# Deferred numerators in a linear-attention phase, and the edges' gathers and scatters regrouped in tiles of 128

## The reference, cut to what matters

```python
# graph attention of layer 0, over 21250 edges (src, dst); 4 heads of 64
xl = (x @ Wl).reshape(n, H, D); xr = (x @ Wr).reshape(n, H, D)
msg = xl[src] + xr[dst]
act = where(msg > 0, msg, 0.2 * msg)
e = einsum('ehd,hd->eh', act, att)          # one score per edge and head
...                                          # softmax over the edges of a node
# mix, 16 heads of 64
q = phi(x @ Wq); k = phi(x @ Wk); v = x @ Wv
kv = einsum('bhtd,bhtm->bhdm', k, v)
num = q @ kv; den = q @ k.sum(t)
out = (num / den) @ Wo
```

## Time and profile before

| | us |
|---|---|
| median of three runs | 3459.63 |
| the profiled execution, its own time | 3469.89 |
| its span in the profile | 3468.2 |
| count, 124 to 402 | 278 |
| mix0, 402 to 938 | 536 |
| out0, 938 to 1172 | 234 |
| mix1, 2221 to 2645 | 424 |
| PE busy over the span | 2749.8 (79%) |
| DVE busy | 1617.4 (47%) |
| POOL busy | 916.4 (26%) |

### The profile page before, as it was taken

One profiled execution on the slowest core, in us unless ns is written; L12 is line 12 of the kernel. 1 busy time (PEld: TensorE's weight loads), 2 busy tenths in 40 slices (PEclk: granted clock), 3 DMA queues, 4 the chain that ended last, 5 costly groups with the idle time before them and its releaser, 6 DMA issues. The chain is left out here.

```text
span 3468.2 us, 53667 instructions
## 1 busy us (share of the span) xinstructions
PE 2749.8 (79%) x19204; PEld 2534.2 (73%) x19204; DVE 1617.4 (47%) x3435; ACT 870.3 (25%) x1619; POOL 916.4 (26%) x790
## 2 busy tenths in 40 slices
PE   4757587887686399459994999899998979996468
PEld 3534487887676398358884999899997969995257
DVE  6668455455553388465555222233334322224445
ACT  3100132332210156215432100134342120002033
POOL 0166476677656322112210000000000001000154
PEclk7978798998888689659996999899998989997579
DMA  9722333332364696517745211110112461114064
GB/s 225 189 67 68 88 87 87 79 90 73 91 149 104 149 220 167 173 44 202 202 121 140 76 40 40 52 51 26 51 45 81 127 179 56 58 59 138 2 226 148
DMA packets 251509, 370.39 MB, mean 107 GB/s; under 512 B 64744, under 2 KB 193792, under 8 KB 250095
## 3 DMA queue, kind: packets, MB, share of 16 engines
q1 hardware_dynamic: 187457, 287.84, 29.4%
q0 software_dynamic: 63888, 80.33, 10.1%
HBM read 279.45 MB, written 99.41 MB: 109 GB/s over the span
## 5 line engine op out<-in xcount | busy, mean ns | idle before, releaser
L308 PE MATMUL mix_bank<-mix_wkv_hi,layer_act_hi 128*125 128x256 f32 x1280 | 359.4, 281 | 0.0
L309 PE MATMUL mix_bank<-mix_wkv_lo,layer_act_hi 128*125 128x256 f32 x1280 | 359.3, 281 | 0.0
L310 PE MATMUL mix_bank<-mix_wkv_hi,layer_act_lo 128*125 128x256 f32 x1280 | 359.0, 280 | 0.0
L498 POOL DMA_INDIRECT scores<-edge_e,edge_now x170 | 218.2, 1284 | 233.0 <-issue 162.9
L486 POOL DMA_INDIRECT edge_gl<-xl,edge_now x170 | 212.0, 1247 | 171.6 <-issue 169.5
L309 PEld LDWEIGHTS mix_bank<-mix_wkv_lo,layer_act_hi 128*125 128x125 f32 x1280 | 237.7, 186 | 0.1
L310 PEld LDWEIGHTS mix_bank<-mix_wkv_hi,layer_act_lo 128*125 128x125 f32 x1280 | 237.7, 186 | 0.0
L308 PEld LDWEIGHTS mix_bank<-mix_wkv_hi,layer_act_hi 128*125 128x125 f32 x1280 | 237.3, 185 | 0.1
L486 POOL DMA_INDIRECT edge_gr<-xr,edge_now x170 | 214.7, 1263 | 51.9 <-issue 34.8
L308 PE MATMUL out_bank<-out_w_hi,layer_act_hi 128*125 128x256 f32 x640 | 191.1, 299 | 36.5 <-DVE out_w_lo L1617 26.2
L775 PE MATMUL count_pa<-count_hot_s,count_hot_d 125*125 125x416 bf16 (+1 forms) x624 | 146.1, 388 | 68.6 <-DVE count_hot_s L718 66.6
(11 more groups left out here) (509 smaller groups left out, 7654.8 us busy)
## 6 DMA issues: line engine op xcount, KB each, us to landing
ffn_raw<-in_L_ffn_w_dram SPq DMA_DIRECT2D x16, 2048.0 KB
scores<-targets_hole SPq DMA_DIRECT2D x40, 546.9 KB
gat_sc<-scores SPq DMA_DIRECT2D x10, 2187.5 KB
block_raw<-in_L_ffn_W_dram SPq DMA_DIRECT2D x16, 1024.0 KB
norm_x<-x SPq DMA_DIRECT2D x30, 448.0 KB
mix_raw<-in_L_mix_w_qkv_dram SPq DMA_DIRECT2D x24, 512.0 KB
sage_cnt<-at SPq DMA_DIRECT2D x20, 546.9 KB
out_part<-mixt SPq DMA_DIRECT2D x16, 625.0 KB, 4.6
```

Source lines behind the costliest of these rows:

```text
L308: pe.matmul(out, lhs[0], rhs[0], start=first, stop=False)
L309: pe.matmul(out, lhs[0], rhs[1], start=False, stop=False)
L310: return pe.matmul(out, lhs[1], rhs[0], start=False, stop=last)
L498: pool.indirect_dma_start(self.scores, bass.IndirectOffsetOnAxis(ap=self.now[:, u % (2 * RING), 2, j:j + 1].bitcast(U32), axis=0), self.e[ ...
```

## The change

It has four parts.

1. Numerators deferred. The mix phase loses its loops and becomes one flat list over all slabs. The numerators of slab g - 1 are computed after `q` 0 of slab g. `pair` comes after `q` 1 and 2; the weights are prepared in the order 4, 5 (query), then `pair`, then 0 to 3, and loaded in the order Wq, Wk, Wv. This holds for mix0 and mix1.
2. Edges in tiles of 128. The 21250 edges are 166 full columns of 128 and 2 left over; the last two columns repeat known edges around the 2 left. This makes 168 columns, 84 batches, 66 of them up to the end of mix0 and 18 in out0.
3. Scores held, and the queue's order. All scores stay in SBUF (`e`), so a scatter can come later than its step; indices are read in place, `now` and its copies go. POOL's turn for batch b issues, per column, gather, gather, scatter. The gathers of batch b + 2 wait for the step of b - 1 (before: b). Scatters and diagonal lag 8 batches behind until batch 18, and catch up by one batch per turn in the turns of batches 19 to 25.
4. Slope split. leaky(m) . att = 0.2 m . att + 0.8 max(m, 0) . att. The linear part comes out of `proj` as 4 more columns of `xl` and `xr` (rows of 260 values, 1040 bytes), by small products with `lin` (six on PE for each tile of nodes); the step becomes add (260 wide), max-times-att, reduce, add of 4 values per edge.

```diff
+BATCHES = -(-EDGE_COLS // EB) + 1
-AHEAD = 3
+AHEAD = 2
+LAG = 8
...
+    def written(self, b):
+        return max(0, b + 1 - max(1, LAG - max(0, b - COUNT_BATCHES)))
...
+        for b in range(first, end):
+            done = range(self.written(b - 1) if b else 0, self.written(b))
+            if 0 in done:
+                self.diagonal(pool)
+            for j in range(EB):
+                if b + AHEAD < BATCHES:
+                    self.gather(pool, b + AHEAD, j)      # waits s_e >= b + 2 - RING + 1
+                for d in done[:1]:
+                    self.scatter(pool, d, j)             # waits s_e >= d + 1, s_sc of the one before
+            for d in done[1:]:
+                for j in range(EB):
+                    self.scatter(pool, d, j)
...
         link(dve.tensor_tensor(gl, gl, gr, ALU.add))
-        link(dve.scalar_tensor_tensor(gl, gl, 0.2, gl, ALU.mult, ALU.max))
-        link(dve.tensor_tensor(gl, gl, e.attb[:, :].unsqueeze(1).to_broadcast([R, EB, HID]), ALU.mult))
-        dve.tensor_reduce(e.e[:, slot, :, :], gl.rearrange("p t (a d) -> p t a d", a=HEADS), AX.X, ALU.add)
+        link(dve.scalar_tensor_tensor(gl[:, :, 0:HID], gl[:, :, 0:HID], 0.0,
+                                      e.attb[:, :].unsqueeze(1).to_broadcast([P, EB, HID]), ALU.max, ALU.mult))
+        link(dve.tensor_reduce(score, gl[:, :, 0:HID].rearrange("p t (a d) -> p t a d", a=HEADS), AX.X, ALU.add))
+        dve.tensor_tensor(score, score, gl[:, :, HID:], ALU.add).then_inc(e.s_e, 1)
...
-    steps = [("q", 0)] + [("kv", t) for t in range(T)] + \
-            [("w", 0), ("w", 1), ("q", 1), ("w", 2), ("w", 3), ("pair", 0), ("q", 2), ("w", 4), ("w", 5)] + \
-            [("n", j) for j in range(NC)]
+    flat = [(-1, "w", c) for c in W_ORDER]               # W_ORDER = (4, 5, 0, 1, 2, 3)
+    for g in range(SLABS):
+        flat += [(g, "q", 0)]
+        flat += [(g - 1, "n", j) for j in range(NC) if g]
+        flat += [(g, "kv", t) for t in range(T)] + [(g, "q", 1), (g, "q", 2)]
+        flat += [(g, "w", c) for c in W_ORDER[:2] if g + 1 < SLABS] + [(g, "pair", 0)]
+        flat += [(g, "w", c) for c in W_ORDER[2:] if g + 1 < SLABS]
+    flat += [(SLABS - 1, "n", j) for j in range(NC)]
```

More of the change, by code:

```diff
@@ L489, in gpsimd @@
-    def gpsimd(self, pool, first, end):
[L491 to L494, removed]
-            for j in range(EB):
[L496 to L507, removed]
-                for j in range(EB):
[L509 to L522, removed]
@@ new lines, in vector, with turns, at, gather @@
+        dve.tensor_copy(idx[:, 2, :], idf[:, 1, :]).then_inc(self.s_cell, 1)
+        dve.wait_ge(self.s_att, 16)
+        link(dve.tensor_scalar(self.attb[:, :], self.attb[:, :], 1.0 - SLOPE, None, ALU.mult))
+        dve.wait_ge(self.s_cell, 1)
+    def turns(self, dve, first):
+        return EdgeTurns(self, dve, first)
+    def at(self, j, k):
+        return bass.IndirectOffsetOnAxis(ap=self.idx[:, j, k:k + 1].bitcast(U32), axis=0)
+    def gather(self, pool, b, j):
+        slot = b % RING
+        if b >= RING and j == 0:
+            pool.wait_ge(self.s_e, b - RING + 1)
+        for row, (buf, x) in enumerate(((self.gl, self.xl), (self.gr, self.xr))):
+            pool.indirect_dma_start(buf[:, slot, j, :], None, x, self.at(row, EB * b + j)).then_inc(self.s_g[slot], 16)
@@ new lines, in scatter, with diagonal @@
+    def scatter(self, pool, b, j):
+        if j == 0:
+            pool.wait_ge(self.s_e, b + 1)
+        k = EB * b + j
+        pool.wait_ge(self.s_sc, 16 * (T + 1) + 16 * k)
+        pool.indirect_dma_start(self.scores, self.at(2, k), self.e[:, k, :], None).then_inc(self.s_sc, 16)
+    def diagonal(self, pool):
+        pool.wait_ge(self.fill.s_fill, self.fill.count)
+        flat = self.scores.rearrange("s h -> (s h)")
+        diag = flat[0:(N * N - 1) * HEADS].rearrange("(i x) -> i x", x=(N + 1) * HEADS)
+        for t in range(T):
+            n = min(R, N - 1 - t * R)
+            pool.dma_start(diag[t * R:t * R + n, 0:HEADS], self.loops[0:n, t, :]).then_inc(self.s_sc, 16)
+        pool.dma_start(self.scores[N * N - 1:N * N, :], self.loops[R - 1:R, T - 1, :]).then_inc(self.s_sc, 16)
@@ L523, in gpsimd, with __init__ @@
         if end == BATCHES:
-            pool.wait_ge(self.s_sc, self.stored(end))
+            for d in range(self.written(end - 1), end):
+                for j in range(EB):
+                    self.scatter(pool, d, j)
+            pool.wait_ge(self.s_sc, 16 * (T + 1) + 16 * ET)
 class EdgeTurns:
-    def __init__(self, edges, dve, first, g):
-        self.edges, self.dve, self.first, self.g = edges, dve, first, g
-        self.u = first if g is None else 0
+    def __init__(self, edges, dve, first):
+        self.edges, self.dve, self.u = edges, dve, first
@@ L1319, in _ @@
                     dve.wait_ge(s_bq, 16)
-                at = {}
-                for c in range(WCHUNKS):
-                    weights(c + 1, c, c % 4)
+                    dve.tensor_scalar(bias_less[:, :], bias_q[:, :], -1.0, None, ALU.mult)
+                    dve.tensor_scalar(bias_more[:, :], bias_q[:, :], 1.0, None, ALU.add).then_inc(s_both, 1)
+                    dve.wait_ge(s_both, 1)
                 dve.wait_ge(s_zero, 1)
-                at = banks(steps)
-                with dve.Fori(0, SLABS - 1) as g:
-                    slab(g, steps)
-                at = banks(last_steps)
-                slab(SLABS - 1, last_steps)
+                todo = edges.turns(dve, COUNT_BATCHES) if edges is not None else None
+                for i in range(len(flat) + 2):
+                    if i < len(flat):
+                        start(*flat[i])
+                    first = 2 <= i and flat[i - 2][1] == "pair"
+                    if first:
+                        finish(*flat[i - 2])
+                    if 1 <= i <= len(flat):
+                        middle(*flat[i - 1])
+                    if i >= 2 and not first:
+                        finish(*flat[i - 2])
+                    if todo is not None and i < len(flat) and flat[i][1:] in EDGE_AFTER:
+                        todo.step()
                 dve.wait_ge(s_den, 1)
```

462 lines of the change are left out of this document (219 added, 243 removed).

## The result

The changed kernel takes 3291.62 us (median of 4 runs, 3281.08 to 3295.51) against 3459.93 (4 runs): ratio 0.9509, 95% interval 0.9484 to 0.9533, 168 us less. The forecast was 3334 with the range 3290 to 3385. The time lies in the range, at its low end: the change gave 168 us where 126 were forecast. The profiled execution took 3295.51 us with a span of 3293.8.

A forecast was written before the change was run, and what follows sets the result against it. The prediction saw PE held by late sums behind POOL's long transfer queue, and out0 by the edges. Count -46, mix0 -41, out0 -29, mix1 -12, front +2 sum to -126: 3344 profiled, 3334 median, range 3290 to 3385.

The forecast's parts named there:

- Mix0: Stage mix0: PE's waits for sums go, POOL's queue becomes the limit; -41 us, bounds -10 to -95.
- A transfer of 128 rows I price at 1.54: POOL's queue in mix0: 1.54 us per transfer against 1.52 before, so 9.24 us per batch.
- Count: Stage count: shorter edge step 11 us, VectorE's waits 24.6, earlier end 10.8; sum -46, least -20.
- PE the limit in mix0: Rival for mix0: cheaper transfers give POOL slack, 54 us less, total 3280; chance 0.04.
- Numerators: Mix0: with `q` 0 and four transposes between sums and numerators, PE's wait of 9.1 us per slab goes.
- Out0: Stage out0: fewer transfers and gathers no longer a step late end the scatters earlier; -29 us.
- Mix1: Stage mix1: slabs lose 8.6 us of PE waiting in all, first product starts sooner; -12 us, from -6 to -15.
- Front: Stage before count: six more small products per node tile, mostly hidden; +2 us, from -2 to +8.
- Landings fast: Rival for mix0's catch-up and out0: scatters land before the next could start; total 3301, chance 0.20.
- Late first gathers: Rival for count: the 24.6 us of VectorE's waits stay; total 3358, chance 0.07.
- landings slow: Rival for mix0 and out0: extra scatters land slowly and out0 keeps its pace; total 3378, chance 0.15.
- dearer transfers: Rival for mix0 and out0: issuing 128 rows costs more; at 1.90 us each the kernel takes 3476; chance 0.03.

The follow-up runs named there:

- e2: Changed kernel with edges in tiles of 127 rows instead of 128; 4413.68 us, ratio 1.2711 to the kernel before.
- e1: Changed kernel with edges in tiles of 125 rows again, all else as changed; 3393.48 us, ratio 0.9785 to the kernel before.
- e12: Kernel before with edges in tiles of 128 rows and nothing else changed; 3378.93 us, ratio 0.9733.
- e6: Changed kernel with scatters one batch behind their step from the start instead of eight, on the chip with pauses; 3434.96 us, ratio 0.9905 to the kernel before.
- e4: Changed kernel with the slope in one piece again, without the small products in the front; 3295.46 us, ratio 0.9492 to the kernel before.
- e3: Changed kernel with each slab's numerators back at the slab's end; 3300.46 us, ratio 0.9509 to the kernel before.
- e9: Changed kernel untouched, measured a third time, on a chip without pauses; 3290.34 us, ratio 0.9493 to the kernel before.
- first and third group: Follow-ups that met no pauses in mix0: first, parts of the change undone (e1 to e4); third, on another chip, including e9, e10 and e12; ratios 0.9460 to 1.2711.
- second group: Follow-ups on the chip with pauses: changed kernel untouched (e5) and three edits of its catch-up, e6 among them; ratios 0.9845 to 0.9905 to the kernel before.
- e5: Changed kernel untouched, measured again on the chip with pauses; 3429.19 us, ratio 0.9894 to the kernel before.
- e10: Changed kernel with TensorE's program for slabs 2 to 6 of the mix stages as a loop; 3306.31 us, ratio 0.9541 to the kernel before.

## Why the prediction was right in sign and short in size

The prediction had the sign and four of five terms within 9 us. That the time lies in the range is in part luck: it is 1.6 us above the lower end, and single runs go down to 3281. Inside the profiled execution, where the sums were made, 3344 was forecast and 3295.5 measured, 48.5 us less, and the range reached down only 44. Its lower end stood for faster landings, which did not come, and not for a cheaper issue.

 **The step that failed is the price of a transfer in "Mix0": "A transfer of 128 rows I price at 1.54".** It measured 0.95 to 0.99 plus 0.30, some 1.27 (3.81 / 3). The price came from direct transfers of 1 and 125 rows, 513 and 531 ns, which did not carry over to an indirect one: POOL's time for that fell by a fifth with three rows more, and one row less than 128 costs 2.6 times as much (e2). e1 and e12 show what it is worth from both sides: rows alone 90 us, all the rest 75. The rule of the Trainium skill that the prediction named, page "DMA: Bandwidth & Descriptors", section "Why a DMA increments its semaphore by 16 and not by 1", gives 16, 5 and 1 engines for 128, 125 and 127 rows. Packets and prices rise in that order (36,432, 63,888, 202,608; 0.97, 1.23, 2.56 us), so the traces agree with it; which engines ran, they do not show, and the rule says nothing of the issue's price. The rule was used for the landing alone, where it gave little.

Term by term:

- *Count, -46, measured -50.2.* e6 gives up to 16.6 us of it to holding the scores (on the chip with the pauses). VectorE has no wait for gathers over 2 us after the first tiles and POOL is no longer last, as forecast. The 11 us for the shorter step are not there: e4 gives 2.6. Rows alone take 17.3, which the sum did not have; it overlaps with the rest.
- *Mix0, -41, measured -78.2.* The forecast made POOL the limit at 55 us a slab; PE is the limit at 52.7. That is the rival "PE the limit in mix0", held at 0.04, and for the cause it named, cheaper transfers; it asked for 95 us and got 78, since the catch-up remains, 22 us in its slab. The prediction also kept PE at the old clock; with fewer waits the clock rose from 0.90 to 0.97, worth 15 us of PE's time. The queue's model was too cheap besides. At the old price (e1) the stage fell by 8.9 us, not 41: catch-up turns took 16.6 us instead of 15.2 (7 x 1.4 = 10) and ordinary ones 9.81 instead of 9.24 (39 x 0.57 = 22). In e1's catch-up POOL waits 30.9 us for scatters to land, and in the 39 turns 11.4 us for landings and 6.0 us for steps of VectorE, a wait that the prediction said nobody would meet. The earlier trace rows are one turn without such waits. So two errors of opposite sign met.
- *Numerators.* That PE's 9.1 us a slab go was right, and so was the reason: with the old rows the new order takes the wait from 64.0 us to 5.3 (e1), though VectorE still waits 118 us for gathers in that mix0. But it gave the stage only 8.9 us, because POOL set the pace there. Rows alone take half of the wait (e12), as VectorE is less late. So the wait needed both, a late VectorE and the old order. What the old order would cost with cheap transfers was not run, since e3 undoes only a part of it in mix0.
- *Out0, -29, measured -37.9.* Within its bounds (-16 to -42), by rows for the greater part: 26.5 in e12, 12.8 in e1.
- *Mix1, -12, measured -12.6.* e3 puts 9.7 of it on the numerators, where 8.6 were forecast. The slabs take 49.8 us against 49.3 forecast and 50.5 before.
- *Front, +2, measured +5.2* (and 3.4 in e9), inside -2 to +8; e4 takes 4.3 away with the small products.

"Landings fast" gave the nearest time of all rivals (3301), but not by its mechanism: in the catch-up the extra scatters still start 2.9 and 2.4 us behind the one before. "Late first gathers", "landings slow" and "dearer transfers" did not come.

The prediction also named code that arrives late at an engine. In the first trace and in those of the first and third group there is no sign of it. On the chip of the second group PE pauses without a wait, only in stages where POOL's transfers run beside it, and the kernel before lost nothing (3467.55 us). For late code speaks that the kernel before loops over the slabs (7 packets of code in mix0), where the changed one fetches 24. Against it speak two stages of e5: mix1 fetches 22 packets and has no pause, and count fetches 3 (the kernel before 2) and has 25 us of them. A rival is that the transfers of 128 rows disturb PE there and those of 125 do not; it was not run. The cause is open: e10, made to test late code, met a chip without pauses.

## What to carry to other kernels

Try the number of rows of an indirect transfer before anything else: 128 instead of 125 was worth more than all the rest of the change (90 against 75 us), and with 127 the changed kernel was 945 us slower than the kernel before. The price rose as the largest divisor up to 16 fell (16, 5 and 1 for 128, 125 and 127); no other numbers were run. Price a queue from many of its turns, those that meet waits among them, and spread a backlog over turns that have slack instead of paying it in a row. Undo a part of a change in every stage where it acts before calling it cheap: the same edit undid the order in mix1 and only a part of it in mix0. Time a rewrite on several chips before its gain is believed: here the same kernel gained 5% in two measurements and 1% in a third, on another chip.

## What the runs showed of the hardware that was not expected

- POOL's own time for an indirect gather of about 1 KB a row is 0.97 us for 128 rows, 1.23 for 125 and 2.56 for 127 (medians); the gap between two is 0.30 us with each.
- The packets of the whole queue go from 36,432 to 63,888 and 202,608 for nearly the same bytes (80.98, 81.01 and 85.05 MB).
- Landing follows less: in the catch-up, scatters behind scatters start 2.4 to 3.0 us apart with 128 rows and 2.7 to 4.5 with 125.
- On one chip PE paused in trains 1.4 or 2.1 us apart, 56 us in mix0 that nothing in the trace accounts for, at unchanged transfer prices; at the lower clock (0.90 against 0.97) its products took 36 us more.
